# A graph network's edge loop in blocks of 256 edges and eight buffers in place of 512 edges and four

## The reference

```python
def _transformer_conv(x, edge_index, Wq, bq, Wk, bk, Wv, bv, Ws, bs):
    q, k, v = ...                                  # N x 4 heads x 16
    logits = (q[dst] * k[src]).sum(-1) * (1.0 / np.sqrt(C))
    m = jax.ops.segment_max(logits, dst, num_segments=N)
    e = jnp.exp(logits - m[dst])
    denom = jax.ops.segment_sum(e, dst, num_segments=N)
    alpha = e / (denom[dst] + 1e-16)
    out = jax.ops.segment_sum(v[src] * alpha[..., None], dst, num_segments=N)
    return out + x @ Ws.T + bs

h = relu(_transformer_conv(layernorm(x), ...))     # layer 0
h = relu(_transformer_conv(h, ...))                # layer 1
x = x + sigmoid(h @ Wo.T + bo)
x = x + experts(layernorm(x))                      # 8 dense experts, three layers each
```

## Time and profile before

| | before |
|---|---|
| median of 3 runs | 3429.82 us (3421.93 to 3433.68) |
| profiled execution | 3430.09 us, span 3428.2 us |
| busy, share of the span | PE 71%, PEld 61%, DVE 67%, ACT 41%, POOL 54% |
| mean granted TensorE clock | 0.751 |
| HBM traffic | 246.63 MB read, 110.66 MB written |
| packets on DMA queues | 365,085 |

### The profile page before, as it was taken

One profiled execution on the slowest core, in us unless ns is written; L12 is line 12 of the kernel. 1 busy time (PEld: TensorE's weight loads), 2 busy tenths in 40 slices (PEclk: granted clock), 3 DMA queues, 4 the chain that ended last, 5 costly groups with the idle time before them and its releaser, 6 DMA issues. The chain is left out here.

```text
span 3428.2 us, 47561 instructions
## 1 busy us (share of the span) xinstructions
PE 2429.0 (71%) x13194; PEld 2093.5 (61%) x13194; DVE 2287.0 (67%) x3449; ACT 1402.9 (41%) x2768; POOL 1850.0 (54%) x1956
## 2 busy tenths in 40 slices
PE   1537666666666665466666667666499999999999
PEld 1425555555555554355555555455489988999998
DVE  3347777777777763577777777777556655666655
ACT  7312333233233321133333333333366766766665
POOL 6577777777777767777777777777300000000000
PEclk9756666666666655576666666666599999999999
DMA  9544444454444432455455545455200000000000
GB/s 374 186 111 132 137 133 136 129 138 134 134 132 135 135 74 74 123 139 141 137 144 139 144 136 141 138 141 138 67 15 17 8 26 12 15 25 11 11 12 12
DMA packets 365085, 358.64 MB, mean 105 GB/s; under 512 B 58803, under 2 KB 297698, under 8 KB 364982
## 3 DMA queue, kind: packets, MB, share of 16 engines
q1 hardware_dynamic: 192326, 170.48, 16.0%
q0 software_dynamic: 62832, 125.63, 15.0%
q10 hardware_dynamic: 109824, 61.36, 5.9%
HBM read 246.63 MB, written 110.66 MB: 104 GB/s over the span
## 5 line engine op out<-in xcount | busy, mean ns | idle before, releaser
L164 POOL DMA_INDIRECT kv<-kv_table,ix x1664 | 1585.5, 953 | 507.1 <-issue 507.1
L615 PE MATMUL kT<-identity,kv 128*128 128x128 f32 x832 | 357.9, 431 | 822.6 <-DMA kv<-kv_table,ix 822.6
L615 PEld LDWEIGHTS kT<-identity,kv 128*128 128x128 f32 x832 | 182.6, 219 | 844.2 <-issue 685.8
L709 ACT ACTIVATE drop<-rise 128x512 f32<-128x512 f32 x208 | 131.0, 630 | 1267.0 <-DVE rise L685 1267.0
L665 DVE TENSOR_TENSOR_SCAN held_q<-mask,held_q,qT 128x512 f32<-128x512 bf16 x208 | 266.2, 1280 | 505.0 <-PE qT L616 503.2
L1411 DVE TENSOR_TENSOR hid_lo_x<-full_x,hid_hi_x 128x448 fp32r<-128x448 f32 x448 | 276.1, 623 | 250.2 <-ACT hid_hi_x L1284 245.7
L1284 ACT ACTIVATE full_x<-psH_x,offset_x,scale_x 128x448 f32<-128x448 f32 x448 | 333.1, 744 | 256.1 <-PE psH_x L1137 256.1
L622 PE MATMUL logit<-kq,head_sum 128*128 128x512 f32 x416 | 386.2, 1031 | 0.6 <-DVE rise L685 0.6
L1085 POOL DMA_DIRECT2D x_x<-in_x x7 | 6.8, 972 | 628.7 <-DVE total_x L1457 489.3
L616 PE MATMUL qT<-identity,qz 128*128 128x128 f32 x832 | 345.7, 416 | 0.0
L639 PE MATMUL restT<-pick,top 128*128 128x8 f32 x1664 | 335.5, 274 | 0.0
(11 more groups left out here) (231 smaller groups left out, 5411.5 us busy)
## 6 DMA issues: line engine op xcount, KB each, us to landing
running_sums<-rows ACTq DMA_DIRECT2D x208, 288.0 KB
qz<-q_at_starts SPq DMA_DIRECT2D x208, 256.0 KB, 3.2
mask<-masks SPq DMA_DIRECT2D x416, 128.0 KB, 3.4
q_at_starts<-zeros SPq DMA_DIRECT2D x16, 1664.0 KB, 18.8
kv<-kv_table,ix POOLq DMA_INDIRECT x1664
x_sb<-in_x SPq DMA_DIRECT2D x1, 6272.0 KB, 27.6
kv_table<-proj SPq DMA_DIRECT2D x14, 448.0 KB, 3.2
x_x<-in_x POOLq DMA_DIRECT2D x7, 896.0 KB, 5.8
```

What stands on the lines that cost most here:

```text
L164: pool.indirect_dma_start(kv[:, b % UNROLL, j, 2 * HC * s:2 * HC * (s + 1)], None, kv_t, bass.IndirectOffsetOnAxis(ix[:, b, n:n + 1], 0)). ...
L615: pe.transpose(kT[u % 2][:, P * j:P * (j + 1)], kv[:, u, j, 0::2], identity[:, :])
```

## The change

The block is halved: 256 edges of each stream, two tiles, four gathers, 208 blocks, eight buffers. The number of gathers, turns of the loop, edges in flight and bytes is the same; `TAIL_BLOCKS` and `EARLY` are doubled so that they mean the same edges. The masks are computed in one instruction on 104 rows as before, each row now holding a pair of blocks, so their arrays have one more dimension.

```diff
-TAIL_BLOCKS = 8
+TAIL_BLOCKS = 16
...
-STEP = 512
+STEP = 256
 TPB = STEP // P
-UNROLL = 4
+UNROLL = 8
 BLOCKS = -(-E // (STREAMS * STEP * UNROLL)) * UNROLL
 STEPS = BLOCKS // UNROLL
 ALL_STORED = 16 * BLOCKS // 2
-EARLY = 1
+EARLY = 2
...
-            dst_b = sb("dst_b", [BLOCKS, STREAMS, STEP], I32)
-            prev_b = sb("prev_b", [BLOCKS, STREAMS, STEP], I32)
-            mask_b = sb("mask_b", [BLOCKS, STREAMS, 2, STEP], BF16)
+            PAIRS = BLOCKS // 2
+            dst_b = sb("dst_b", [PAIRS, STREAMS, 2, STEP], I32)
+            prev_b = sb("prev_b", [PAIRS, STREAMS, 2, STEP], I32)
+            mask_b = sb("mask_b", [PAIRS, STREAMS, 2, 2, STEP], BF16)
...
-                            sp.dma_start(mask_t[s], mask_b[:, s, :, :].rearrange("b m c -> b (m c)")).then_inc(masks_out, 16)
+                            sp.dma_start(mask_t[s].rearrange("(b k) c -> b (k c)", k=2),
+                                         mask_b[:, s, :, :, :].rearrange("b k m c -> b (k m c)")).then_inc(masks_out, 16)
...
-                last = sum_t[EP - 2 * STEP * TAIL_BLOCKS:EP, :].rearrange("(p k n) c -> p k (n c)", p=P, k=TAIL_BLOCKS // 2)
-                sp.dma_start(last, zeros[:, 0:16 * ROW].unsqueeze(1).to_broadcast([P, TAIL_BLOCKS // 2, 16 * ROW])).then_inc(cleared_out, 16)
+                last = sum_t[EP - 2 * STEP * TAIL_BLOCKS:EP, :].rearrange("(p k n) c -> p k (n c)", p=P, k=TAIL_BLOCKS // 4)
+                sp.dma_start(last, zeros[:, 0:16 * ROW].unsqueeze(1).to_broadcast([P, TAIL_BLOCKS // 4, 16 * ROW])).then_inc(cleared_out, 16)
```

More of the change, by code:

```diff
@@ L268, in _ @@
                 sp.dma_start(samples_i[:, :], d["samples"].partition_broadcast(P)).then_inc(samples_in, 16)
-                sp.dma_start(dst_b[:, :, :], d["dst"].rearrange("(s b c) -> b s c", s=STREAMS, c=STEP)).then_inc(edges_in, 16)
-                sp.dma_start(prev_b[:, :, :], d["prev"].rearrange("(s b c) -> b s c", s=STREAMS, c=STEP)).then_inc(edges_in, 16)
+                sp.dma_start(dst_b[:, :, :, :], d["dst"].rearrange("(s b k c) -> b s k c", s=STREAMS, k=2, c=STEP)).then_inc(edges_in, 16)
+                sp.dma_start(prev_b[:, :, :, :], d["prev"].rearrange("(s b k c) -> b s k c", s=STREAMS, k=2, c=STEP)).then_inc(edges_in, 16)
                 sp.dma_start(x_sb[:, :, :], d["x"].rearrange("(i p) c -> p i c", p=P)).then_inc(x_in, 16)
@@ L413, in _ @@
                 dve.wait_ge(edges_in, 32)
-                step(dve.tensor_tensor(mask_b[:, :, 0, :], dst_b[:, :, :], prev_b[:, :, :], ALU.is_equal))
-                step(dve.memset(mask_b[0:1, 1, 0, 0:1], 0.0))
-                step(dve.tensor_scalar(mask_b[:, :, 1, :], mask_b[:, :, 0, :], -NEG, NEG, ALU.mult, ALU.add))
+                step(dve.tensor_tensor(mask_b[:, :, :, 0, :], dst_b[:, :, :, :], prev_b[:, :, :, :], ALU.is_equal))
+                step(dve.memset(mask_b[0:1, 1, 0, 0, 0:1], 0.0))
+                step(dve.tensor_scalar(mask_b[:, :, :, 1, :], mask_b[:, :, :, 0, :], -NEG, NEG, ALU.mult, ALU.add))
                 dve.sem_inc(masks_made, 1)
```

## The result

| | before | after |
|---|---|---|
| median of 9 runs each, same chip | 3425.94 us (3420.55 to 3433.68) | 3439.98 us (3438.76 to 3441.15) |
| ratio to before, 95% interval | | 1.0042 (1.0032 to 1.0052) |
| profiled execution | 3430.09 us, span 3428.2 | 3438.76 us, span 3436.8 |
| busy | PE 71%, DVE 67%, ACT 41%, POOL 54% | PE 81%, DVE 73%, ACT 46%, POOL 54% |
| mean granted TensorE clock | 0.751 | 0.67 |

A forecast was written before the change was run, and what follows sets the result against it. The edge loop was taken as bound by POOL's 1664 gathers, 1.257 us apart. Shorter layer ends, 11.2 + 11.0 = 22.2 us, off the profiled 3430.09 give 3407.9, or 3407.6 us as a median; range 3394 to 3424.

The forecast's parts named there:

- POOL in the loop: nothing: Edge loop: gathers stay 1.257 us apart; the 208 more waits cost nothing, or 4 us at 0.02 us each.
- DVE under cover: Edge loop: DVE's half pass takes 4.34 us, under the 5.03 us in which four gathers supply it.
- rival D: Edge loop: DVE becomes the bound if scans save under 0.38 us; slower, 3456 to 3590 us. Chance 0.12.
- The closings: Ends of both edge layers, last gather to last store: shrink to 18.6 us, gaining 11.2 and 11.0 us.
- Rival B: Layer 0's end: POOL's 21 gathers of results hold the barrier, only 5 us gained there, 3414 us. Chance 0.05.
- C: Layer ends: uneven landings leave a backlog and the closings don't shrink, 3418 to 3430, say 3425 us. Chance 0.15.
- wrong altogether: Sign of failure: a changed gather time, or an expert stage whose length is no longer 975 us.
- PE in the loop: nothing: Edge loop: PE's half pass takes some 4.4 us even at its lower clock, under the 5.03 us supply.

The follow-up runs named there:

- a_flat3: The changed kernel with PE's expert loop written out as seven groups, on a chip where the kernel before takes 3426.14 us: 3396.8 us, 0.9916 of it.
- b_flat2: The kernel before with PE's expert loop written out as seven groups, on a chip where the unaltered one takes 3426.14 us: 3421.0 us, 0.9984 of it.
- a_flat: The changed kernel with PE's expert loop written out as seven groups, on a chip where the kernel before takes 3836.27 us: 3892.63 us, 1.0159 of it.
- b_flat: The kernel before with PE's expert loop written out as seven groups, on a chip where the unaltered one takes 3836.27 us: 3832.21 us, 0.9987 of it.
- a_dve57: The changed kernel with 114 waits (57 instructions) at the head of DVE's expert program: 3978.94 us, 1.0295 of the kernel before on that chip.
- a_pe128: The changed kernel with 256 waits (128 instructions) at the head of PE's expert program: 3948.95 us, 1.0231 of the kernel before on that chip.

## Why the prediction was wrong

**POOL in the loop: nothing.** Right: 952 ns and 507.3 us of idle for 1664 gathers. 3.7 us of that idle are waits on PE (507.3 - 503.6), inside the 4 us allowed. PE's part holds too: it is 83% busy in the middle of the loop and waits 432.2 us for `kv` in all.

**DVE under cover, rival D.** Right, and D is out. The scans over 256 columns take 0.743, 0.748, 0.740 and 0.724 us (held_q, before, run_d, run_v on the page), that is, 0.53 to 0.54 saved where I took 0.55; a tensor-tensor 0.42, so 0.27 saved. The half pass above runs from 828.54 to the start of its last scan at 832.29, and that scan takes 0.72: 4.47 us at most, where 4.34 was summed and 5.03 is the supply. The Trainium skill's page "DVE: opcode table, instruction layouts, handler registers and perf-mode slots" (section "6. Datapath and trigger behaviour") says that the built-in scan runs at half throughput. The estimate of 0.53 us worked out from it agrees with the trace.

**The closings.** Right. Forecast 18.6 us from last gather to last store in both layers, measured 18.2 and 18.9; forecast 22.2 us of gain, measured 23.6 in the profiled run and 24.2 as the difference of a_flat3 and b_flat2. Rival B is out (the scatter came 10.7 us earlier, not 5), and C too. Layer 0 got its gain although POOL's gathers of results ran on.

**The step that failed** is one that was never priced. The change was costed engine by engine inside the edge phases, and the expert stage was taken over at its 975 us; the text names its length only at the very end, as what would make it "wrong altogether". The part "PE in the loop: nothing" counts matmuls and not instructions of the list: the two edge phases, written out for blocks of half the size, put 200 more instructions in front of a later stage's loop. That moved its 1791 instructions to a place where PE must fetch them again at every jump back, 8.4 us a turn (41.8 over 5 turns), of which 6.7 us is standing still (33.3 us of "issue" over 5); the rest goes, by its size, to the matmuls behind it at the lower clock. The kernel before paid 10.2 us for this in its profiled execution, the changed one 41.9. 23.6 gained and 32.2 lost are the 8.6 us by which the two spans differ.

The hint was in the trace of before: one turn of 139.3 us among turns of 131 to 134; two waits of PE on "issue" (6.6 us) in a stage that is otherwise without any; and instruction transfers that come nine in one turn (2767 to 2906) and none in another (3037 to 3169). A stage whose equal turns take unequal times depends on something that is not in its code.

The Trainium skill's page "Runtime: NRT & Kernel Launch" (section "Instruction fetch mechanics") says that PE's instruction memory is a queue of 128 KiB, 2048 instructions, filled in blocks of 16 KiB, and that crossing a block costs little. The runs agree for code that is run straight on: a_flat's 54 transfers cost nothing that shows. The same section of the Trainium skill says that a taken branch whose target is not in the current window of two blocks must wait until that block is fetched, and names this as a reason to write code out. The changed kernel agrees: both waits at each of its five jumps, and nine transfers in each turn (2478 to 2618, 2618 to 2758, and so on), where a_flat3 running straight on makes six or seven. The kernel before agrees only in part: its loop is seven blocks long too, so by that rule each of its five jumps would wait, and three did not.

The chance of 0.12 for "slower" was put on DVE, which was not the cause.

**The best version.** The change with PE's expert groups written out, a_flat3: 0.9916 (0.9901 to 0.993) of the kernel before and some 43 us under the changed kernel, where landings are early. Where they are late it is slower than the kernel before (1.0147 to 1.0159), and of the kernels tried only b_flat holds its time there.

## What to carry to other kernels

Writing out more code in one stage can slow a loop in a later stage on the same engine. Compare the distances between equal turns in every stage, also in those that a change leaves alone: a turn that is longer by some us, idle on "issue" behind the jump back, and a block of "instruction" transfers with it is code being fetched again. A loop of about 1800 instructions on PE was cheaper written out: 42 us over five turns in the changed kernel, 5 us in the median of the kernel before, which missed fewer jumps.

## What the runs showed of the hardware

- Straight code of 12,500 instructions on PE (the seven groups written out) ran at 131 to 132 us a group in a_flat3 and 132 to 134 in a_flat, without a gap of over 0.8 us on "issue". A jump back over 1791 instructions cost nothing, 1 to 3 us (one wait, clock still 1.00 behind it: the turn of 133.6 in the kernel before) or 7 to 10 us (turns of 139.3 to 140.7). On the chips with late landings it was about 10 us and more with two waits (143.3 in a_dve57 against 132.2 to 133.9 in a_flat) and less with one (136.3 to 139.8 in a_pe128).
- Whether it costs depends on the place of the loop: with the loop at 2361 and 2617 only some jumps cost (two of five in each trace), at 2561, 2689 and 2816 all do.
- Behind 7 us of idle PE ran for 5 us at a granted clock of 0.52, before it was 1.00 again.
- The second code transfer behind a jump starts when the packets of SP's store of `out` (896 KB) end, to within 0.01 us, at all five jumps of the changed kernel; the DMA share is 0.41 in 2744 to 2751. Whether the store delays the fetching, and a store at another time would shorten the wait of 4.4 us, was not tried.
- The same kernel takes 3426 us on some chips of the same kind and 3832 to 3870 on others, and the change, with PE's expert groups written out, helps on the former and hurts on the latter.
